# A last layer's row variances computed in the feed-forward stage, its row normalisation on ScalarE, and a reordered recurrent slot, in a one-core transformer block

## What is computed

```
def mingru(x, Wz, bz, Wh, bh):
    z = sigmoid(x @ Wz.T + bz);  t = tanh(x @ Wh.T + bh)
    return linear_scan(clip(1 - z), z * t)            # along the tokens
def stack(x):                                         # L = 4 layers
    h = x
    for i in range(4):
        hn = mingru(h, ...)
        if i > 0: hn = hn + h
        h = layernorm(hn) * gamma + beta
h_comb = concat(stack(n(x)), flip(stack(flip(n(x)))))   # n: layernorm without weights
x = x + h_comb @ fusion_W.T + fusion_b
h = gelu(n(x) @ ternary(W_fc).T)                        # 2048 hidden
x = x + (layernorm(h) * ln_w + ln_b) @ ternary(W_proj).T
```

## Time and profile before

| | before |
|---|---|
| median of 3 runs (lowest to highest) | 1538.08 us (1537.69 to 1538.49) |
| the profiled execution: its time, its span | 1538.64 us, 1536.8 us |
| PE busy | 1515.5 us, 99% |
| DVE busy | 1318.8 us, 86% |
| ACT busy | 1021.6 us, 66% |
| POOL busy | 829.7 us, 54% |
| granted TensorE clock | full in all 40 slices |
| HBM traffic, mean | 73 GB/s |

### The profile page before, as it was taken

One profiled execution on the slowest core, in us unless ns is written; L12 is line 12 of the kernel. 1 busy time (PEld: TensorE's weight loads), 2 busy tenths in 40 slices (PEclk: granted clock), 3 DMA queues, 4 the chain that ended last, 5 costly groups with the idle time before them and its releaser, 6 DMA issues.

```text
span 1536.8 us, 22966 instructions
## 1 busy us (share of the span) xinstructions
PE 1515.5 (99%) x7744; PEld 1197.1 (78%) x7744; DVE 1318.8 (86%) x2038; ACT 1021.6 (66%) x1688; POOL 829.7 (54%) x1013
## 2 busy tenths in 40 slices
PE   9999999999999999999999999999999999999998
PEld 6877888888888888888888877777777777777766
DVE  8998999999899988999888887787887877777786
ACT  7988889898687898787987444545454444445364
POOL 5766657678868678676788632241323333332231
PEclk9999999999999999999999999999999999999999
DMA  4211212321302112222143551030202020111000
GB/s 172 76 34 70 93 66 89 120 75 63 123 31 95 41 56 73 79 96 83 35 144 126 197 186 42 1 110 1 90 21 89 21 90 21 62 48 45 25 22 35
DMA packets 73157, 113.20 MB, mean 74 GB/s; under 512 B 5193, under 2 KB 37961, under 8 KB 69970
## 3 DMA queue, kind: packets, MB, share of 16 engines
q1 hardware_dynamic: 72754, 111.21, 21.2%
q10 hardware_dynamic: 288, 0.52, 0.1%
HBM read 73.95 MB, written 37.77 MB: 73 GB/s over the span
## 4 chain that ended last, share of the span: by engine, by line
PE 49%; DVE 3%; ACT 1%; issue 0%; POOL 0%; DVEq 0%; POOLq 0%; ACTq 0%
PE ps L640 15%; PE ps L621 14%; PE ps L572 11%; PE ps L501 6%; PE ps L521 1%; PE ps L586 1%; PE ps L535 1%; DVE bnp L1131 1%; ACT H L875 0%; PE ps L650 0%; DVE yb L1111 0%; DVE H L1119 0%; ACT AH L879 0%; DVE H L1120 0%; DVE ps L1099 0%
## 5 line engine op out<-in xcount | busy, mean ns | idle before, releaser
L501 PE MATMUL ps<-AH,WH 128*128 128x512 f32 x896 | 367.1, 410 | 7.8 <-DVE H L1120 6.1
L501 PE MATMUL ps<-AL,WH 128*128 128x512 f32 x896 | 351.1, 392 | 0.0
L501 PE MATMUL ps<-AH,WL 128*128 128x512 f32 x896 | 349.7, 390 | 0.0
L1604 POOL TENSOR_TENSOR H<-H,yb 128x512 f32<-128x512 f32 x192 | 246.0, 1291 | 8.5 <-DVE yb L1111 1.3
L1111 DVE TENSOR_TENSOR_SCAN yb<-ab,ps 128x512 f32<-128x512 f32 x192 | 232.1, 1209 | 15.5 <-POOL ab L1595 9.1
L949 ACT ACTIVATE g<-ps 128x512 f32<-128x512 f32 x128 | 76.5, 598 | 245.2 <-PE ps L621 245.1
L836 ACT ACTIVATE yb<-ps,ncnd 128x512 f32<-128x512 f32 x224 | 158.1, 706 | 87.9 <-PE ps L501 84.9
L501 PEld LDWEIGHTS ps<-AH,WH 128*128 128x128 f32 x896 | 168.6, 188 | 46.6 <-DVE H L1120 8.6
L1705 POOL TENSOR_TENSOR rs<-mv,nhalf 128x1 f32<-128x1 f32 x32 | 43.0, 1342 | 286.4 <-DVE mv L1278 286.4
L501 PEld LDWEIGHTS ps<-AL,WH 128*128 128x128 f32 x896 | 168.2, 188 | 37.0
L501 PEld LDWEIGHTS ps<-AH,WL 128*128 128x128 f32 x896 | 169.1, 189 | 29.4
(11 more groups left out here) (195 smaller groups left out, 3230.4 us busy)
## 6 DMA issues: line engine op xcount, KB each, us to landing
hs_scratch<-H SPq DMA_DIRECT2D x16, 1024.0 KB, 5.4
hc<-hs_scratch SPq DMA_DIRECT2D x32, 512.0 KB, 4.5
xr<-in_x SPq DMA_DIRECT2D x32, 256.0 KB, 4.6
out<-ob SPq DMA_DIRECT2D x32, 256.0 KB, 2.2
xbuf<-in_x SPq DMA_DIRECT2D x7, 1024.0 KB, 7.8
RAW<-in_wt SPq DMA_DIRECT2D x16, 256.0 KB, 7.3
stg<-in_fct SPq DMA_DIRECT2D x16, 256.0 KB, 3.1
stg<-in_pjt SPq DMA_DIRECT2D x16, 256.0 KB, 2.7
```

The lines of the kernel that those rows point to most:

```text
L501: r = e.matmul(GATE[i % 3][:], w[:, q, m * 128:(m + 1) * 128], a[:, q, :], start=(n == 0), stop=(n == 11))
L1604: e.tensor_tensor(H[s][:, m, :], H[s][:, m, :], yb[i % 5][:], ALU.add).then_inc(s_v, 1)
```

## The change

- `turned(t)` is false for the last layer of batches 2 to 7 (`LATE` = 8 is the first unit concerned). For these 12 tails `tokens`, `stats` and `inv` are left out, in the stack and, for the very last tail, at the FFN's opening.
- Their variances come in the FFN from the units' states, which are loaded for the fusion anyway. Per unit u of 8 to 31: ACT squares the 1024 state elements (`state_squares`), DVE sums states and squares over the four feature chunks of each direction (`state_sums`, twice), transposes 32x32 blocks of the 512 sums and adds up within blocks (`state_blocks`), PE adds over the partition blocks (`stat_sums`, 4 matmuls of 4 columns into TURNED), DVE makes two variances of it in four small instructions (`factors`), POOL takes the power (`state_factors`). The steps are given by `SQUARED_AT`, `SUMMED_AT` and `ADDED_AT`.
- `unit_norm` moves from DVE to ACT, with its bias -mean/deviation by a further small POOL instruction.
- FFN's opening: `fuse(4, 0)` and `resid(4, 0)` come before the steps, the column sums `sums` from the opening to step 4. The loads of states run one unit further ahead and are issued apart from those of rows.
- The slot of the stack has another order on all engines, and its tables with it.

```diff
+SQUARED_AT = {9: 8, 14: 9, 3: 6, 6: 7}
+SUMMED_AT = {10: 8, 1: 5, 4: 6, 7: 7}
+ADDED_AT = {13: 8, 4: 5, 7: 6, 10: 7}
...
-RING_SLOT = [("B", "x", -2, 2), ("B", "b", 3, 2), ("B", "f", 2, 2), ("B", "f", 2, 0), ("B", "f", 2, 1),
-    ("B", "x", -1, 0), ("B", "b", 3, 3), ("B", "f", 2, 3), ("B", "b", 3, 1), ("B", "x", -1, 1), ("B", "b", 3, 0),
+RING_SLOT = [("B", "x", -2, 2), ("B", "b", 3, 2), ("B", "b", 3, 3), ("B", "f", 2, 2), ("B", "x", -1, 0),
+    ("B", "f", 2, 0), ("B", "f", 2, 1), ("B", "b", 3, 1), ("B", "f", 2, 3), ("B", "x", -1, 1), ("B", "b", 3, 0),
...
+LATE = 8
+
+
+def turned(t):
+
+    return t[2] < 3 or 4 * t[0] < LATE
...
         def tokens(tau, pr):
 
-            if tau is None:
+            if tau is None or not turned(TAILS[tau]):
                 return
...
+        def stat_sums(u):
+
+            b, n = (u - 4) // 4, u - LATE
+            e.wait_ge(f_hs, 4 * n + 4)
...
+            for c in range(4):
+                r = e.matmul(TURNED[32 * c:32 * c + 32, 0:4], sel[:], hpart[:, :, c], start=True, stop=True)
+            r.then_inc(f_ht, 1)
...
             fc(j)
             if b > 0 and c == 1:
                 moments(b - 1)
-            if b + 1 < NB and c in FUSE_AT:
+            if unit_at(b, c, ADDED_AT) is not None:
+                stat_sums(unit_at(b, c, ADDED_AT))
+            if b + 1 < NB and c in FUSE_AT and j > 2:
...
+            e.activation(hsq[:], hc[i][:], ACT.Square).then_inc(f_hq, 1)
...
+            e.activation(n1[:], x1[u % NX1][:], ACT.Identity, bias=nun[:, r:r + 1], scale=rs[:, r, 0:1]).then_inc(f_n1, 1)
...
+        def state_sums(u, of_squares):
+
+            n = u - LATE
+            src = hsq if of_squares else hc[u % 2]
...
+            e.reduce_sum(hsum[:, 2 * of_squares:2 * of_squares + 2, :], src[:].rearrange("p (d q) t -> p d t q", d=2),
+                         axis=AX_X).then_inc(f_hs, 1)
...
+            e.transpose(hturn[:].rearrange("p k t -> p (k t)"), hsum[:].rearrange("p k t -> p (k t)")).then_inc(f_hs, 1)
+            e.wait_ge(f_hs, 4 * n + 3)
+            e.reduce_sum(hpart[:], hturn[:].rearrange("p k (b j) -> p k b j", j=32), axis=AX_X).then_inc(f_hs, 1)
...
+            if unit_at(b, c, ADDED_AT) is not None:
+                factors(unit_at(b, c, ADDED_AT))
...
             total(j)
             squares(j)
+            if unit_at(b, c, SUMMED_AT) is not None:
+                state_sums(unit_at(b, c, SUMMED_AT), 0)
+                state_sums(unit_at(b, c, SUMMED_AT), 1)
+                state_blocks(unit_at(b, c, SUMMED_AT))
...
+            e.tensor_tensor(rl[:, u // 4, :, u % 4], hvar[:, r, :], nhalf[:, 0:2], ALU.pow).then_inc(f_rl, 1)
```

More of the change, by code:

```diff
@@ L172 @@
         _i = subject(_who, _s - _o)
-        if _i is not None and _what == "T":
-            USERS += [("T", _i, _n, 0), ("T", _i, _n, 1)]
+        if _what == "T":
+            USERS += [] if _i is None or not turned(TAILS[_i]) else [("T", _i, _n, 0), ("T", _i, _n, 1)]
         elif _i is not None and (_who == "x" or TAILS[_i][2] < 3):
@@ L327, in pixart_block @@
     xh.append(sb(p2, "xh1", [128, KC, S], F32R))
-    glx = sb(p2, "glx", [128, 4, S], F32R)
+    with ExitStack() as p4:
+        glx = sb(p4, "glx", [128, 4, S], F32R)
+    with ExitStack() as p5:
+        hsq = sb(p5, "hsq", [128, 8, 128])
+        hsum = sb(p5, "hsum", [128, 4, 128])
+        hturn = sb(p5, "hturn", [128, 4, 128])
+    sb(p2, "under", [128, 4, S])
     gh = [sb(p2, f"gh{i}", [128, S], F32R) for i in range(3)]
@@ L391, in pixart_block @@
     s_gb, s_ws = sem("s_gb"), sem("s_ws")
+    f_hq, f_hs, f_ht, f_hv, f_rl, f_un = (sem(n) for n in ("f_hq", "f_hs", "f_ht", "f_hv", "f_rl", "f_un"))
     f_bt, f_bs, f_sl = sem("f_bt"), sem("f_bs"), sem("f_sl")
@@ L567, in fuse @@
                 e.wait_ge(s_sc, 4 * NJ)
+            if u == 5 and h == 0:
                 e.wait_ge(f_cs, 1)
@@ L750, in _ @@
             mm(job(s), 1)
+            if s == SUM_SLOT:
+                add_up()
+            back("h", tail_b(s - 3), 3)
             back("h", tail(s - 2), 2)
+            back("x", batch(s + 1), 0)
             back("h", tail(s - 2), 0)
             back("h", tail(s - 2), 1)
-            back("x", batch(s + 1), 0)
-            back("h", tail_b(s - 3), 3)
-            back("h", tail(s - 2), 3)
             mm(job(s), 2)
             back("h", tail_b(s - 3), 1)
+            back("h", tail(s - 2), 3)
             back("x", batch(s + 1), 1)
@@ L762, in _ @@
             tokens(tail_b(s - 1), 0)
+            tokens(tail_b(s - 2), 1)
             mm(job(s), 3)
-            tokens(tail_b(s - 2), 1)
             tokens(tail(s - 1), 1)
@@ L778, in _ @@
         feat(2)
-        tokens(LAST, 0)
-        tokens(LAST, 1)
-        sums(0)
+        fuse(4, 0)
         feat(3)
         fc_three_tiles()
-        sums(1)
         for j in range(NB * NC):
@@ L1080, in _ @@
             hidden(j)
+            if b + 1 < NB and c - 2 in FUSE_AT:
+                unit_norm(4 * b + 4 + FUSE_AT.index(c - 2))
+            if unit_at(b, c, SQUARED_AT) is not None:
+                state_squares(unit_at(b, c, SQUARED_AT))
             if b > 0 and c == 2:
@@ L1496, in _ @@
             input_stats(batch(s + 2))
+            blend(job(s - 2), 3)
+            centred(s)
             if s == ABS0 + 16:
                 sums_abs()
-            if s == 57:
-                cut(0)
+            scan(job(s - 2), 3)
+            blend(job(s - 1), 0)
+            scan(job(s - 1), 0)
+            if s == 8:
+                bias_rows(1)
+            low("h", tail_b(s - 4), 2)
+            if s == 24:
+                thresholds()
             if s == 58:
                 cut(1)
[L1503 to L1508, removed]
             blend(job(s - 1), 1)
[L1510 to L1513, removed]
         resid(0, 0)
@@ L1788, in _ @@
         for s in SLOTS:
+            inv(tail(s - 4), 1)
+            if s == 58:
+                addx(0)
+            keep(job(s - 3), 3)
             add(job(s - 3), 1)
-            inv(tail(s - 4), 1)
-            keep(job(s - 3), 3)
             keep(job(s - 2), 0)
-            inv_x(batch(s + 1))
             add(job(s - 3), 2)
@@ L1798, in _ @@
             pieces(s - 1)
-            add(job(s - 2), 0)
+            inv_x(batch(s + 1))
             inv(tail(s - 3), 0)
-            if s == 58:
-                addx(0)
             keep(job(s - 2), 2)
             inv(tail_b(s - 4), 1)
+            add(job(s - 2), 0)
             inv(tail_b(s - 3), 0)
@@ L1820, in _ @@
                 inv_2(b - 1)
-            if j in (4, 7):
-                whole_row((4, 7).index(j))
+            if unit_at(b, c, ADDED_AT) is not None:
+                state_factors(unit_at(b, c, ADDED_AT))
+            if j in (9, 10):
+                whole_row((9, 10).index(j))
             if b + 1 < NB and c - 1 in FUSE_AT:
@@ L2003, in _ @@
                 spread_sums()
-            if u + 5 < NU and u + 5 > 4:
-                load_unit(u + 5)
+            if u + 6 < NU:
+                load_states(u + 6)
+            if u + 5 < NU:
+                load_rows(u + 5)
             if u >= 4:
```

180 lines of the change are left out of this document (128 added, 52 removed).

## The result

The changed kernel takes 1605.14 us (median of 3 runs, 1604.11 to 1605.28), 1.043 times the time before [1.041 to 1.0458]: slower, as forecast, but 29 us beyond the forecast and 17 us outside the range. The profiled execution took 1605.28 us with a span of 1603.3 us.

The account below looks back on a forecast made before the run. PE was taken to bound the kernel. Transposes -21.1, stack waits -2, opening -1, small matmuls +9.1 and FFN waits +53 gave +38.0 on 1538.64, so 1576 us after 0.56 to the median; range 1529 to 1588.

Parts of the forecast that it names:

- The sums' price: DVE in the FFN: each of two sums over 1024 elements per unit takes 2.09 us, from strided reading.
- the lower bound: DVE's sums in the FFN: 1.24 us for 1024 elements if they run at the rate of contiguous elements.
- the 378 ns instruction: DVE's existing sum at L1352, four elements far apart per result, 128 elements; taken as nearest row for pricing the new sums.
- The full rate for odd strides: DVE's sums in the FFN run at the contiguous rate, 1.24 us each; time 1526 to 1537; rival's chance 0.27.
- place A: FFN steps 1 and 2, DVE's block ahead of `resid(u, 0)`: PE waits 1.56 us, in each of 6 batches.
- B: FFN steps 4 and 5, DVE's block ahead of `resid(u, 0)`: PE waits 3.15 us, in each of 6 batches.
- C: FFN steps 7 and 8, DVE's block ahead of `resid(u, 0)`: PE waits 2.63 us, in each of 6 batches.
- D: FFN steps 10 and 11: PE waits 1.53 us in each of 6 batches, after 2.05 us of stretching is given back.
- the second rival: DVE's rows in the FFN stay stretched beside POOL's two-input additions: waits cost 65 us, time 1588; chance 0.10.
- the main step: PE's waits in the FFN are lost one for one: 8.9 us per batch, 6 batches, +53 us.
- the second step: The stack: fewer PE waits with DVE relieved and the slot reordered, -2 us, between -8 and +8.
- The third rival: The slot's new order makes new waits in the stack, PE idle some 8 us more; time about 1541; chance 0.05.

Follow-up runs that it names:

- contiguous_sums: The changed kernel with the two sums reading four neighbouring elements per result instead of four 512 bytes apart (sums of other elements than wanted): 1563.15 us, ratio 1.0164.
- filled_wait: The changed kernel with 18 unused matmuls put into PE's longest wait in each of batches 1 to 6, 108 in all: 1596.15 us, ratio 1.0378.
- adds_after_resid_old_order: The changed kernel with additions for the strided sums, their block behind `resid(u, 0)`, and the stack's slot order of before: 1530.86 us, ratio 0.9955, the fastest.
- old_slot_order: The changed kernel with the stack's slot and its tables in the order of before: 1599.53 us, ratio 1.0401.
- adds_for_sums: The changed kernel with the sums computed by additions of whole contiguous rows in two levels, at the same place: 1566.86 us, ratio 1.0186.
- sums_after_resid: The changed kernel with the block of sums put behind `resid(u, 0)` instead of just ahead of it: 1568.4 us, ratio 1.0199.

## Why the prediction was wrong

*Right.* The sums' price: 2.09 forecast, 2.03 and 1.99 measured, and the contiguous run gives 1.21 where the lower bound was 1.24. The choice of the nearest row, the 378 ns instruction, was the decisive one and held. The penalty for another 16-byte line (the Trainium skill, SBUF — State Buffer, Door 1) agrees with 2.01 against 1.21 us. The full rate for odd strides, which the prediction drew from the Trainium skill, VectorE: DVE Perf Modes (Mode 1×), does not hold for this sum: 1.9 ns per element against 1.05. `stat_sums`: from the last `fc` pair to the second `proj` matmul it is 1.04 us with it (1102.50 to 1103.54 in filled_wait), 0.66 without: 0.38, as forecast. The block, its four places and the 24 waits are all there.

*The waits, nearly right, in part by luck.* PE's idle time in brackets understates a wait, since a matmul's end is modelled. Without a wait the second fusion matmul stands 0.66 us behind the last `fc` pair (1106.51 to 1107.17 above). At place A of the fourth batch it stands 1.98 us behind, so the wait costs 1.32 where 1.08 is printed: 0.24 more. In the same way, in that batch:

| place | forecast, us | measured, us |
|---|---|---|
| A | 1.56 | 1.32 |
| B | 3.15 | 3.99 |
| C | 2.63 | 1.85 |
| D | 1.53 | 1.35 |

(At B the half clock would count into this reading, so there it is the first matmul's start, 4.34 us behind the pair, less the 0.35 by which A's 1.67 exceeds 1.32.) B is longer since the running sum is stretched there (1.75 us at 1097.32), which the second rival had as its mechanism; A, C and D are shorter. And the first wait of all, at D of the first batch, was 4.0 us where the later ones at D were 1.1, which no term had. These errors cancel in part. (The working also took 0.32 us between two rows of step 4 that lie 0.37 apart, 0.05 us per place.) The total is 49.6 + 24 x 0.24 = 55.4 us against 53.

*Wrong, the main step: "whatever makes PE wait is lost one for one".* A long wait also costs pace behind it. adds_after_resid_old_order gives the floor: 677.3 us of FFN (851.5 to 1528.8) with all new work on PE, none of these waits, and one wait of 1.3 us for the first normalised row that the other runs have too. Against that floor:

| | FFN, us | over floor | waits (idle + 0.24 each) | added matmuls | left over | at half clock | of it PE busy |
|---|---|---|---|---|---|---|---|
| after | 748.9 | 71.6 | 55.4 | | 16.2 | 41 | 35.9 |
| old_slot_order | 748.4 | 71.1 | 55.5 | | 15.6 | 38 | 34.7 |
| filled_wait | 737.7 | 60.4 | 31.6 | 108 x 0.23 = 24.8 | 4.0 | 10 | 10.2 |
| contiguous_sums | 706.9 | 29.6 | 20.7 | | 8.9 | 20 | 20.5 |
| adds_for_sums | 708.2 | 30.9 | 25.0 | | 5.9 | 10 | 10.2 |
| sums_after_resid | 712.3 | 35.0 | 35.0 | | 0.0 | 0 | 0 |

What is left over goes with the time at half clock. At one matmul per 0.43 us instead of 0.23, each microsecond that PE works at half clock loses 0.47: an estimate of 17, 16, 5, 10, 5 and 0 us for the six rows, within about 1 us of what is left over. So the clock cost about 16 us, and no term of the sum had it.

*Wrong, the second step: the stack's -2 us.* 22 of the 24 calls stand ahead of the first fusion, 19.4 us by the forecast's price; with the -2 it should have begun at 846.3 us and began at 854.4: 8 us. PE's idle time in the stack did not fall by 2 us, it grew by 4 (15.3 to 19.3): 6 of the 8 us. By runs, the new order costs 3.6 us of this (old_slot_order). The other 4.5 are there in the old order too: its 850.7 stands against 848.3 for the saved calls alone, so the relief of 2 did not come, nor 2.4 of the saving; why is not shown. Between -8 and +8 the term was bounded, and +6 is what it measured. That the order costs 11 us where the turnings stay and 3.6 where they go says that its price can't be judged apart from what else stands in the slot. The third rival's mechanism was real, at half its size, and it was given too little weight because the queues showed only moved calls, not what would wait.

*The sum.* 1576.6 forecast, 1605.3 measured in the profiled execution, 28.7 more: stack 8.1, clock 16.2, waits 2.4; the remaining 2.0 holds the new wait of 1.3 us for the first normalised row from ACT (L620).

*Also off:* DVE was to be over 90% busy in FFN. It is at 82% (78.56 of 95.41), because DVE itself stands before the low parts ahead of a block (1.51 us at 1087.35). The fastest kernel has DVE at 92% and no such wait, so a full DVE was no sign of the trouble; 5.3 us in one piece just ahead of the one result that PE needed was.

## What to carry to other kernels

Where a change makes TensorE wait, price the wait and then the matmuls behind it at half clock: here that was 16 us on top of 55. Work that an engine has time for still costs if it stands in one piece ahead of a result that another waits for; move it behind that result and make it cheap (either alone 1567 or 1568 us, both together 1534, in the same slot order, from 1605). And run a reordering by itself: this one cost 13 us on the kernel of before, hidden by a saving in the same diff.

## What the runs showed that was not expected

- The clock fell to 0.50 within a batch that is 92% busy, after waits of 3.7 us, and in contiguous_sums after waits of 2.27 us, all six times. In filled_wait waits of 2.02 us at the same place C were followed by full clock in four batches and by 0.50 in two.
- Sums of four elements 512 bytes apart take 2.01 us for 1024 elements, of four neighbours 1.21; adding contiguous rows in two levels takes 0.68 + 0.41 us where undisturbed.
- In the change's FFN every two-input instruction of DVE on 512 columns that took over 0.9 us, 49 of them, ran beside a two-input addition of POOL; one on 2 columns took 1210 ns on the mean in the fastest kernel (160 in after). The strided sums, with one input, kept to 1.96 to 2.05 us, though 12 of the 48 ran beside such an addition.
